# Expert rows fetched through a table of one-hot sums, and gated units one slot later

## What is computed

```python
def step(state, xs):                      # the scan, per sequence
    d_t, B_t, C_t, u_t = xs
    dA = jnp.exp(d_t[..., None] * A)
    state = state * dA + (d_t * u_t)[..., None] * B_t[:, None, :]
    y_t = jnp.einsum('ben,bn->be', state, C_t)
    return (state, y_t)
...
# experts of layer 0: every token goes to its 4 best of 16, weighted
y = jax.nn.silu(x @ g.T) * (x @ u.T) @ d.T
acc + we[:, None] * y
```

## Time and profile before

| | us |
|---|---|
| median of 3 runs | 1790.8 (1788.43 to 1791.03) |
| the profiled execution | 1789.81 |
| its span | 1788.1 |
| DVE busy | 1522.2 (85%) |
| PE busy | 1310.4 (73%) |
| POOL busy | 833.3 (47%) |
| ACT busy | 775.7 (43%) |

### The profile page before, as it was taken

One profiled execution on the slowest core, in us unless ns is written; L12 is line 12 of the kernel. 1 busy time (PEld: TensorE's weight loads), 2 busy tenths in 40 slices (PEclk: granted clock), 3 DMA queues, 4 the chain that ended last, 5 costly groups with the idle time before them and its releaser, 6 DMA issues.

```text
span 1788.1 us, 13500 instructions
## 1 busy us (share of the span) xinstructions
PE 1310.4 (73%) x4076; PEld 729.8 (41%) x4076; DVE 1522.2 (85%) x1488; ACT 775.7 (43%) x1183; POOL 833.3 (47%) x407
## 2 busy tenths in 40 slices
PE   6566666766677676777529999779998799912868
PEld 2122222322233232332207765557655577712444
DVE  3999999899989999999917987879887899976884
ACT  4545455434543455324304445434455444413342
POOL 0365456635663665337262433634336343465641
PEclk7798789889987998888859999889998899965989
DMA  7485466247534752356657776478765678744431
GB/s 244 118 207 140 139 188 182 79 128 211 165 92 125 205 147 56 96 167 217 189 212 253 273 254 206 138 235 273 233 210 179 202 261 278 274 128 123 125 111 47
DMA packets 128986, 317.74 MB, mean 178 GB/s; under 512 B 12913, under 2 KB 13425, under 8 KB 122769
## 3 DMA queue, kind: packets, MB, share of 16 engines
q1 hardware_dynamic: 118288, 282.78, 51.4%
q0 software_dynamic: 10240, 33.56, 5.6%
q10 hardware_dynamic: 384, 0.52, 0.1%
HBM read 241.85 MB, written 74.97 MB: 177 GB/s over the span
## 4 chain that ended last, share of the span: by engine, by line
DVE 43%; PE 23%; DMA 9%; issue 8%; ACT 8%; POOL 7%; SPq 1%; DVEq 0%; POOLq 0%; ACTq 0%
DVE state L1299 17%; PE banks L913 9%; DVE banks L1291 8%; DMA ys_d<-expert_out 4%; PE banks L923 4%; DMA z_gate<-xs_d 3%; DVE x_res L1474 3%; ACT decay L583 2%; DVE du L1107 2%; DVE small L1141 2%; ACT expert_w L583 2%; POOL state L407 2%; POOL xs_d L454 2%; PE banks L841 2%; PE banks L806 1%
## 5 line engine op out<-in xcount | busy, mean ns | idle before, releaser
L407 POOL TENSOR_TENSOR state<-state,bc_rows 128x1024 f32<-128x1024 f32 x240 | 575.5, 2399 | 766.4 <-DVE banks L1291 766.4
L841 PE MATMUL banks<-state,ident 128*128 128x512 f32 x640 | 356.5, 689 | 209.8 <-POOL state L407 178.8
L1299 DVE TENSOR_TENSOR_SCAN state<-decay,banks 128x1024 f32<-128x1024 f32 x184 | 420.2, 2284 | 6.9 <-ACT decay L583 2.0
L1291 DVE TENSOR_TENSOR banks<-du,bc_rows 128x1024 f32<-128x1024 f32 x256 | 336.3, 1314 | 11.1
L913 PE MATMUL banks<-z_gate,expert_w 128*128 128x256 f32 x1504 | 337.2, 383 | 1.1 <-issue 0.7
L913 PEld LDWEIGHTS banks<-z_gate,expert_w 128*128 128x128 f32 x1504 | 288.5, 192 | 64.2 <-issue 24.1
L841 PEld LDWEIGHTS banks<-state,ident 128*128 128x128 f32 x640 | 124.3, 211 | 418.4 <-POOL state L407 265.0
L583 ACT ACTIVATE decay<-delta,neg_a 128x511 f32<-128x511 f32 x368 | 242.8, 714 | 87.7 <-DVE state L1299 75.4
L923 PE MATMUL banks<-expert_w,hidden 128*128 128x512 f32 x376 | 185.7, 618 | 0.0
L1299 DVE TENSOR_TENSOR_SCAN state<-expert_w,banks 128x1024 f32<-128x1024 f32 x72 | 164.6, 2286 | 2.5
L1316 DVE TENSOR_TENSOR y_scan<-y_scan,state 128x1024 f32<-128x1024 f32 x96 | 141.0, 1472 | 8.1 <-POOL state L407 8.1
(11 more groups left out here) (178 smaller groups left out, 1537.0 us busy)
## 6 DMA issues: line engine op xcount, KB each, us to landing
bc_rows<-bc_d SPq DMA_DIRECT2D x208, 512.0 KB, 5.2
expert_w<-in_moe_w SPq DMA_DIRECT2D x48, 1536.0 KB, 8.8
xs_d<-expert_out SPq DMA_DIRECT2D x94, 256.0 KB, 5.4
z_gate<-xs_d SPq DMA_DIRECT2D x47, 512.0 KB, 7.0
ys_d<-expert_out SPq DMA_DIRECT2D x47, 512.0 KB, 9.6
ctx_t<-in_ctxT SPq DMA_DIRECT2D x8, 512.0 KB, 6.9
x_res<-in_x SPq DMA_DIRECT2D x4, 1024.0 KB, 10.6
xn_d<-y_scan SPq DMA_DIRECT2D x4, 1024.0 KB, 7.2
```

The source lines that it names most:

```text
L407: nc.gpsimd.tensor_tensor(W[:, c % 4], W[:, c % 4], bcast2(BC[:, u, 1, :]), ALU.mult).then_inc(mulc_done, 1)
L841: mm = nc.tensor.matmul(PS[:, m], ID[:, :], W[:, c % 4, m, :], start=False, stop=True, skip_group_check=True)
L1291: nc.vector.tensor_tensor(drive(s), DU[:, s % 2, 2 * h:2 * h + 2, :], bcast2(BC[:, u, 0, :]), ALU.mult).then_inc(mulb_done, 1)
L1299: nc.vector.tensor_tensor_scan(flat(W[:, c % 4]), flat(DAS[c % da_slots(s, i)]), flat(drive(s)), 0.0, ALU.mult, ALU.add).then_inc(scan_don ...
```

## The change

1. The zero fill, the scatter and xs_d are gone. A table IDX says for each slot which token it holds. It is the sum over all 8192 pairs of products of two one-hot rows, made in 8 rounds in turn 2 of stage 4: in each round DVE writes the one-hot rows of 8 columns of pairs (mark_rows, 128x1024), POOL their one-hot chunks times the token number (mark_chunks, 8 instructions of 128x94), and PE adds 8 products of 128x94 into one PSUM bank (index_round). DVE copies the bank in turn 3.
2. A tile's 256 rows come by two indirect DMAs of POOL (gather_rows) straight from xn_d, into two buffers in turn.
3. mul_c of turns 2 and 3 of stage 4 is POOL's.
4. The table takes the bank PRE[1], so dt_proj of stage 5 has one bank. It is done one quarter at a time (dt_one), each after ACT has read out the one before, in units 4 to 7 of turn 2.
5. Slot m carries tile m - 1. Slot 0 has no tile, slot 47 has tile 46.
6. SP's order in a slot is now row of B and C, weights, store. The next stage's first three rows are loaded in the last turn of the stage before.

```diff
+            def mark_chunks(n):
+                pool.wait_ge(split_ready, 1)
+                if n >= 2:
+                    pool.wait_ge(indexed, n - 1)
+                for c in range(PPR):
+                    at = n * PPR + c
+                    ins = nc.gpsimd.tensor_scalar(CHUNKHOT[n % 2][:, c, 0:NCH], COUNT1[:, 0:NCH], CHUNK1[:, at:at + 1],
+                                                  ROWID[:, at % NT:at % NT + 1], ALU.is_equal, ALU.mult)
+                ins.then_inc(chunkhot, 1)
+
+            def gather_rows(j):
+                if j >= 2:
+                    pool.wait_ge(xt_done, 2 * (j - 1))
...
+                for r in range(RT):
+                    at = j * RT + r
+                    nc.gpsimd.indirect_dma_start(
+                        out=rows_of(j)[:, r, :], out_offset=None, in_=xn_d,
+                        in_offset=bass.IndirectOffsetOnAxis(ap=IDX[:, at:at + 1], axis=0)).then_inc(xs_in[j % 2], 16)
...
+                        m = TPS * (s - FIRST_B) + i * BODY + c // 2
+                        if c % 2 == 0 and 1 <= m < NTILE - 1:
+                            gather_rows(m + 1)
...
+            def mark_rows(n):
+                if n >= 2:
+                    dve.wait_ge(indexed, n - 1)
+                else:
+                    dve.wait_ge(xn_stored, 16 * NB)
+                own = ROW1[:, n * PPR:(n + 1) * PPR].unsqueeze(2).to_broadcast([P, PPR, P])
+                nc.vector.tensor_tensor(ROWHOT[n % 2], COUNT1.unsqueeze(1).to_broadcast([P, PPR, P]), own,
+                                        ALU.is_equal).then_inc(rowhot, 1)
...
+            def index_round(n):
+                pe.wait_ge(rowhot, n + 1)
+                pe.wait_ge(chunkhot, n + 1)
+                for c in range(PPR):
+                    mm = nc.tensor.matmul(INDEX, ROWHOT[n % 2][:, c, :], CHUNKHOT[n % 2][:, c, 0:NCH],
+                                          start=(n == 0 and c == 0), stop=(n == ROUNDS - 1 and c == PPR - 1))
+                mm.then_inc(indexed, 1)
...
 # ACT, turn 2 of stage 4
-                if c == 3:
-                    step_abs(p, 0)
-                if c == 5:
+                if c >= 4:
+                    step_abs_one(p, c - 4)
+                if c == 4:
                     shared_tanh(f, 1)
-            step_abs(p, 1)
             step_exp(p)
...
 # DVE, turns 2 and 3 of stage 4
                     unit(s, turn, c)
-                    if c:
-                        mul_c(s, turn, c - 1)
-                    if turn == 2 and c in (1, 5):
-                        shared_hidden(f, c // 5)
+                    if turn == 2:
+                        mark_rows(c)
+                        if c in (1, 5):
+                            shared_hidden(f, c // 5)
+                        if c == 7:
+                            shared_add(f, (0, 1))
```

More of the change, by code:

```diff
@@ L51 @@
 TPS = -(-NTILE // (STAGES - FIRST_B))
-ZROWS = NTILE * RT
-ZCH = -(-ZROWS // NB)
+NCH = NTILE * RT
+PAIRS = TOPK * NT
+PPR = 8
+ROUNDS = PAIRS // PPR
+SWAP = 26
 BIG = 3.0e38
@@ L315, in _ @@
             sp.wait_ge(bc_stored, 16 * FIRST_B)
-            for k in range(2 * HPT):
+            for k in range(HS):
                 load_unit(NB, k)
@@ L443, in _ @@
                         step_sum(s + 1)
-            for i in range(2):
+            def mark_chunks(n):
[7 more added lines that the diff above has]
+                ins.then_inc(chunkhot, 1)
@@ L445, in _ @@
+            for i in range(TURNS):
                 for c in range(HPT):
                     mul_c(NB, i, c)
[L448 to L456 removed]
+                    if i == 2:
+                        mark_chunks(c)
+                    if i == 3 and c == 3:
+                        pool.wait_ge(xn_stored, 16 * NB)
+                        pool.wait_ge(index_ready, 1)
+                        gather_rows(0)
+                    if i == 3 and c == 5:
+                        pool.wait_ge(shgu_done, IT * NB)
+                        gather_rows(1)
@@ L518, in step_abs, with step_abs_one @@
             def step_abs(s, pair):
+                for et in (2 * pair, 2 * pair + 1):
+                    step_abs_one(s, et)
+            def step_abs_one(s, et):
                 if 2 <= s < NB + 2:
@@ L818, in dt_proj, with dt_one @@
             def dt_proj(s, pair):
+                for et in (2 * pair, 2 * pair + 1):
+                    dt_one(s, et)
+            def dt_one(s, et):
                 pe.wait_ge(xdbl_ready, s + 1)
                 pe.wait_ge(ld_dtw, 16 * (lay(s) + 1))
-                for et in (2 * pair, 2 * pair + 1):
-                    if pair and s:
-                        pe.wait_ge(dt_read, ET * s + et - 1)
-                    nc.tensor.matmul(pre_bank(s, et), DTW[2 * NS:, et * P:(et + 1) * P], XDBL[2 * NS:, :],
-                                     start=True, stop=True).then_inc(dt_done, 1)
+                if s == FIRST_B:
+                    pe.wait_ge(dt_read, ET * s + et)
+                elif et >= 2 and s:
+                    pe.wait_ge(dt_read, ET * s + et - 1)
+                nc.tensor.matmul(dt_bank(s, et), DTW[2 * NS:, et * P:(et + 1) * P], XDBL[2 * NS:, :],
+                                 start=True, stop=True).then_inc(dt_done, 1)
             def sum_skip(s, half):
@@ L1428, in _ @@
                             step_relu(p)
+                            shared_add(f, (2, 3))
                         if c == 5:
                             step_sum(p)
-                            shared_add(f, (2, 3))
-                mul_c(s, turn, HPT - 1)
             delta_u(p)
```

214 lines of the change are left out of this document (103 added, 111 removed).

## The result

The changed kernel takes 1918.16 us (median of 4 runs, 1917.95 to 1919.55), the kernel before on the same chip 1790.91: a ratio of 1.0712, interval 1.0693 to 1.073. It is slower by 127 us; the forecast was +61, its range ended at 1885. The direction was right, the size was half. The profiled execution has a span of 1916.2 us, 128.1 more than the earlier trace rows.

The account below looks back on a forecast made before the run. No engine was taken to bind throughout; PE binds the slots, with DVE just behind. Terms 14.5 + 48 + 6 - 13 + 5 + 2 = +62 on 1789.8 gave 1852 us, range 1780 to 1885.

Parts of the forecast that it names:

- Forecast (a): Both new waits bind, in stage 4's loops and for the slots' rows: 1852 us, range 1812 to 1885, chance 0.60.
- Stage 4, +22.4 for +14.5: Start to slot 1's first mul_b: the 46.6 us idle goes, but turn 2's loops cost more, +14.5 us.
- my chain: Stage 4, turn 2, one mul_b's end to the next: 8.7 us waiting for rounds, 14.3 us waiting for the projection.
- 4.7 for delta_u and the last mul_c: Slot 0: these two operations take 4.7 us after stage 4's last scan, before PE's sum.
- The steady slots, +84.5 for +48: Transposes wait for fetched rows, so slots take 13.1 us and not 11.2; about 25 slots give +48 us.
- L: Time from a row fetch's issue to its landing, taken as 5.2 us; hidden below 1.4.
- the 4.3 us: In a slot, PE's time from the start of the transposes to the next tile_in.
- Preparation and boundaries, +19.1 for -2: Slots with preparation: +6 for waits, -13 at both stage boundaries, +5 for POOL's late steps in slots 13 and 14.
- rival (e): POOL's issues also delay mul_c and DVE: over 1885 us, chance 0.06.
- Rival (b): The slots' rows arrive in time and only stage 4's loops remain: 1798 us, chance 0.15.
- Rival (c): Stage 4's loops do not bind, turns 2 and 3 being DVE's own work: 1787 down to 1750 us, chance 0.13.
- Rival (d): Neither stage 4's wait nor the slots' wait binds and the 46.6 us are won: about 1735 us, chance 0.06.

Follow-up runs that it names:

- experiment 11: experiment 2 plus 4 matmuls of 128x512 that nobody reads, in front of each sum of stage 4's turn 2 from the second unit on: 1895.4 us.
- experiment 5: Changed kernel with a third buffer for the tile rows, each pair of row fetches being for the tile after next: 1805.8 us.
- experiment 8: Changed kernel with three row buffers, early projection quarters, rounds ahead of sums, turn 2's mul_c on DVE and chunk rows by wide instructions: 1757.8 us.
- experiment 9: experiment 8 with PE's 16 matmuls of the shared expert's second half moved behind the table's third round: 1756.6 us.
- experiment 2: Changed kernel with all four projection quarters made by PE before the units of stage 4's turn 2: 1892.6 us.
- experiment 4: Changed kernel with row gathers moved earlier, projection quarters early as in experiment 2, and turn 2's mul_c on DVE again: 1823.9 us.
- experiment 1: Changed kernel with POOL's two gathers of tile m + 2 put behind the second mul_c of slot m: 1860.0 us.

## Why the prediction was right in its kind and wrong in its size

**The mechanism.** Forecast (a) named the right places: DVE waits for rounds in units 2 to 4, for the decay in units 5 to 7 and the first of turn 3; no idle of tens of us is left before stage 5; transposes wait for their rows. The waits were longer: 9.6 and 5.7 us where I had 4, 12 to 14 where I had 9, and slots of 14.6 us where I had 13. The PE wait of 9.7 us at slot 16 did not vanish: it is 5.4, now for the fetched rows.

**Stage 4, +22.4 for +14.5.** Three things make the 7.9 us that were missing. First the clock. I put 1.2 us on each loop, though the row that I quoted myself had the sum at 3.78 us after 5.2 us of idle. In unit 6 above, sum, round and quarter take 3.6, 2.9 and 1.1 us where my chain had 1.7, 1.9 and 1.1: 2.9 us more, and the loop lasts 17.3 instead of 14.3. The seven loops, from the end of unit 2's mul_b to the end of turn 3's first scan, took 105.0 us where I had 96.8, 8.5 of them for the clock. Of the 8.2 more, 3.7 have the second cause; the other 4.5 are, by difference, the clock. The arithmetic of the loop without the clock was right: 8.7 forecast, 8.69 in experiment 11.

Second, my chain let POOL's mul_c start 0.14 us after the mul_b. In unit 2 POOL was still at its chunk instructions: the eight took 7.46 us while DVE worked beside them, for 5.38 later on while it stood idle. So mul_c started at 825.99 and not at 822.25, 3.7 us late. With 1.1 us gained before the loops, the first scan of turn 3 ended 7.1 us late (927.1 for 920), and turn 3 took back 1.2: of the 3 us that I had booked there for the gathers, 2.3 came, inside another operation (L1163, 4.58 us for 2.28).

Third, L1169 lasts 6.68 us where the same operation had 2.29; my "4.7 for delta_u and the last mul_c" was 2.0 short. 7.1 - 1.2 + 2.0 is the 7.9.

**The steady slots, +84.5 for +48. Here the forecast failed most.** The steps that failed are two terms of the sum 10.9 + L + 10.15 for two slots: L, and the 4.3 us inside the 10.15. The formula for two slots was right in form: second issue at S(m) + 10.8 (forecast 10.9), and 6.0 us from tile_in to the second slot's end (5.85). From the first transpose to tile_in it takes 5.77 us and not 4.3, because after its wait PE runs at the lower clock (0.60 granted in the mean of the first 3.6 us): the first transposes take 1.12 us for 0.60, the next matmuls 2.87 for 1.88. And the landing is 5.8 us in this pair, 6.0 and 7.1 in the median of the two buffers, where I chose 5.2. I had reasoned that longer slots lower the load; they do, from 269 GB/s (experiment 5) to 212, but the landing does not follow: 6.2 there, 6.0 to 7.1 here. The 13 pairs measured average 380.4 / 13 = 29.3 us; less 10.8, 5.77 and 6.0 that leaves 6.7 for the landing, between the two medians. Of the 1.5 us per slot that I lacked (14.6 for 13.1), some 0.7 are the clock and 0.7 the landing. My upper bound of 13.7 us took in the landing but not the clock, so the range was too narrow as well.

The rule that I had set against this, of the Trainium skill (DMA: Bandwidth & Descriptors, section Anatomy of one DMA — SWDGE (gpsimd) path), gives an estimate of 2.6 us for such a fetch; no fetch of the trace landed in under 3.2 us, and the measured median of 6.4 decides.

**Preparation and boundaries, +19.1 for -2.** I said that these slots are bound by other work, and booked 6 us of waiting. It is 22: with the third buffer of experiment 5 the same 20 slots take 318.8 us, for 341.1. Slot 9, for one, went from 14.5 to 20.4 us, and is back at 14.5 there. This is the third term that failed. Slot 15 went from 16.4 to 21.6 us and keeps its 21.6 in experiment 5, so that is not the rows: DVE waits in it twice for POOL's mul_c, which stands behind fetches and a long step.

```profile
1183.27 1.23 DVE L1368 TENSOR_TENSOR y_scan<-y_scan,state 128x1024 f32<-128x1024 f32 x1 [3.74 <-POOL state L405]
...
1194.79 1.23 DVE L1368 TENSOR_TENSOR y_scan<-y_scan,state 128x1024 f32<-128x1024 f32 x1 [3.37 <-POOL state L405]
```

Slots 13 and 14 are 2.8 us shorter together, so the three cost 2.4 us more than before, in each of the two stages (booked 2.5). The boundaries, booked at -13, give -9.7 in experiment 5 (slot 16 lasts 12.2 for 18.0 us and slot 32 13.5 for 17.4) and -7.2 in the changed kernel (14.0 and 14.2).

**The rivals.** The time lies in the region of rival (e), over 1885, but not by its mechanism: experiment 5 has all of POOL's issues and slots of 11.2 us. Rival (b) is what experiment 5 makes true: 1798 forecast, 1805.8 measured. The "2.5 us" of issues in two slots that speak for (b) are those of one slot; two slots have four issues, 5 us. Rival (c) needed turns 2 and 3 to be DVE's own pace, and they took 154 us. Rival (d), 1735, is not what this change does; experiments 8 and 9, with other code in turn 2, come within 22 to 23 us of it.

**Where the gain went.** The scatter's 46.6 us of idle are gone. The change paid for them with two waits of its own. The one for the rows can be removed (experiment 5), the one in turn 2 mostly: the turn takes 64 to 65 us in experiments 8 and 9, for 99.4, and 40.2 before the change, when it made no table. With a third buffer, the projection early and the round first, the same idea is faster than the kernel before by 0.95%; with experiment 8 or 9 by 1.7 to 1.9%. These gains are small, but their intervals leave out a ratio of 1.

## What to carry to other kernels

When a change makes PE wait once per loop, price what follows the wait at the lower clock, in full: take it from a row that stands behind such a wait. Check as well what the engine that the chain runs through still has in hand when the loop begins, as POOL had its chunks. When a load is moved to where it is issued late, look for the smallest buffer that lets it be issued one step ahead before counting the microseconds of its landing; a fetch issued at another place also meets other traffic, so its landing has to be read anew. And if an experiment's gain in one stage is given back in the next, remove the later wait first, then measure again.

## What the runs showed of the hardware

- Filling PE's idle time with useless matmuls made the necessary ones faster: the sum took 1.98 us for 3.78 with 1.5 us of idle left in front of it, at a granted clock of 1.00 for 0.50 (experiments 11 and 2).
- The 6.68 us of L1169 are in the main a wait, which the profile counts as busy time of the instruction. POOL's timeline of the changed kernel has two mul_c at that moment:

```profile
963.66 4.64 POOL L402 TENSOR_TENSOR state<-state,bc_rows 128x1024 f32<-128x1024 f32 x2
```

They end at 968.30, and DVE's operation 2.16 us after that, about its own 2.29. The Trainium skill (SBUF — State Buffer, section SBUF: two separate sides) describes an exclusive lock between the two engines, held for a whole instruction. These rows agree in that DVE's 2.29 us begin only when POOL is done, though DVE waited here through two of POOL's instructions and not one. It also goes the other way round: POOL's 8 chunk instructions take 5.38 us while DVE stands idle (changed kernel) and 8.24 while it works (experiment 4).
- The landing of a fetch of 256 KB in 128 rows does not follow the mean load alone: 6.2 us at 269 GB/s, 6.0 and 7.1 at 212, 8.0 and 5.8 at 229 with the fetches moved, 5.3 and 5.0 at 168. What is issued close to it is the likely rest (experiment 1), which no run here separates.
